# The candidate gate's tanh as an activation of its own, into PSUM, in a recurrence woven through a decoder kernel

## The reference, cut to what matters

```python
def step(carry, xg_t):
    h, c = carry
    g = xg_t + h @ W_hh.T
    i, f, gg, o = jnp.split(g, 4, axis=-1)
    c = jax.nn.sigmoid(f) * c + jax.nn.sigmoid(i) * jnp.tanh(gg)
    h = jax.nn.sigmoid(o) * jnp.tanh(c)
    return ((h, c), h)
```

## Time and profile before

| | us |
|---|---|
| median of 3 runs | 2719.52 |
| lowest, highest | 2716.49, 2726.72 |
| the profiled execution | 2719.7 |
| its span, first to last instruction | 2717.9 |
| PE busy in the span | 2429.8 (89%) |
| DVE busy | 1666.4 (61%) |
| ACT busy | 1296.7 (48%) |
| POOL busy | 1047.2 (39%) |

### The profile page before, as it was taken

The page is one execution under the profiler, slowest core; times in us unless marked ns, Lnnn a source line. Parts: engine busy times, 40 slices in busy tenths (PEclk is TensorE's granted clock), DMA queues, the critical chain, the costliest instruction groups (busy, mean ns, idle before and its releaser), DMA issues. The chain is left out here.

```text
span 2717.9 us, 42457 instructions
## 1 busy us (share of the span) xinstructions
PE 2429.8 (89%) x11677; PEld 1457.4 (54%) x11677; DVE 1666.4 (61%) x6007; ACT 1296.7 (48%) x4633; POOL 1047.2 (39%) x1124
## 2 busy tenths in 40 slices
PE   5799989989999898989999989898988888698887
PEld 2365645535546464636555555555545455466664
DVE  4446466676775766756676767676655646454541
ACT  0263636436364554536364646363543434366642
POOL 0223232122332433333333333333544544487665
PEclk9899999999899999989999999898998889798989
DMA  4301010100202011111202020303343222364324
GB/s 157 95 26 47 26 47 14 44 1 1 84 16 68 17 53 32 44 47 29 62 6 86 9 84 0 99 0 94 97 109 89 78 88 82 93 180 108 90 67 109
DMA packets 203623, 168.32 MB, mean 62 GB/s; under 512 B 56548, under 2 KB 196418, under 8 KB 203153
## 3 DMA queue, kind: packets, MB, share of 16 engines
q1 hardware_dynamic: 189072, 140.73, 17.9%
q0 software_dynamic: 14336, 25.28, 3.2%
HBM read 125.11 MB, written 53.40 MB: 66 GB/s over the span
## 5 line engine op out<-in xcount | busy, mean ns | idle before, releaser
L1163 ACT ACTIVATE l_scratch<-p,l_mx 128x64 f32<-128x64 f32 x2048 | 465.1, 306 | 29.6 <-DVE l_mx L1398 27.5
L951 PE MATMUL pg<-warm 128*64 128x512 bf16 x1528 | 424.7, 411 | 0.0
L1718 POOL TENSOR_TENSOR l_kbd<-l_kg,headmask 128x512 f32<-128x512 f32 x256 | 265.1, 1046 | 384.8 <-PE p L907 289.0
L1703 POOL TENSOR_TENSOR ln_rstd<-ln_ve,neghalf 128x4 f32<-128x4 f32 x96 | 98.2, 1023 | 628.7 <-DVE ln_ve L1360 627.2
L1644 DVE SCALAR_TENSOR_TENSOR uin<-gates 16x20 f32<-16x20 f32 x512 | 202.5, 395 | 206.9 <-ACT gates L1112 192.0
L931 PEld LDWEIGHTS p<-l_vg,l_scratch 128*128 128x128 f32 x2048 | 265.5, 200 | 60.5 <-issue 28.8
L1112 ACT ACTIVATE gates<-pg 16x80 f32<-16x80 f32 x512 | 113.2, 221 | 355.1 <-PE pg L940 343.4
L931 PE MATMUL p<-l_vg,l_scratch 128*128 128x34 f32 x2048 | 271.8, 281 | 8.8 <-ACT l_scratch L1171 4.3
L907 PE MATMUL p<-l_kbd,l_qT 128*128 128x512 f32 x512 | 272.0, 614 | 0.7 <-POOL l_kbd L1718 0.6
L951 PEld LDWEIGHTS pg<-warm 128*64 128x64 bf16 x1528 | 154.5, 115 | 186.5 <-issue 82.2
L940 PE MATMUL pg<-wcat,slots 128*16 128x80 f32 x1024 | 165.1, 244 | 96.7 <-DVE slots L1656 85.0
(11 more groups left out here) (287 smaller groups left out, 4479.2 us busy)
## 6 DMA issues: line engine op xcount, KB each, us to landing
xln<-xln_dram SPq DMA_DIRECT2D x40, 512.0 KB, 4.9
l_vg<-v_dram SPq DMA_DIRECT2D x32, 544.0 KB
x_dram<-l_xres SPq DMA_DIRECT2D x32, 512.0 KB, 4.9
l_kg<-k_dram SPq DMA_DIRECT2D x32, 256.0 KB, 4.2
xln_dram<-l_xnat SPq DMA_DIRECT2D x16, 512.0 KB, 3.9
l_xres<-x_dram SPq DMA_DIRECT2D x16, 512.0 KB
x_dram<-l_xnat SPq DMA_DIRECT2D x16, 512.0 KB
xin<-in_x SPq DMA_DIRECT2D x12, 512.0 KB, 3.8
```

What stands on the lines that cost most here:

```text
L951: pe.matmul(pg[64:128, :], warm[:, 0:64], warm[:, :], start=True, stop=True)
L1163: i = act.activation(w.ex[b % 2][:, NE * j + h, :], banks[lane][j][:, h * SK:(h + 1) * SK], ACT.Exp, scale=-1.0, bias=w.mx[:, u % 4, h:h + 1])
L1718: pool.tensor_tensor(w.kbd[b % 2][:, j, :, :], w.kg[:, j, b:b + 1, :].broadcast_to([P, NE, SK]), headmask[:, :].rearrange("p (a o) -> p a ...
```

## The change

The tanh of the candidate gate is cut out of the activation of all four gates. It gets an activation of its own, ahead of the other, which writes a new region `gate_in` of the PSUM tile `pg`. The other activation has 60 columns instead of 80 and alone signals the semaphore. `uin` reads its second input from `gate_in`. The regions `cell`, `ukept` and `tcell` move within `pg` (from multiples of 128 to multiples of 96) to make room. The planner's cost of the family `tanh` goes from 0.23 to 0.38.

```diff
@@ lstm_steps
-        steps += [("pe", "gates", s, 0.34, [...]), ("act", "tanh", s, 0.23, [("gates", s)]),
+        steps += [("pe", "gates", s, 0.34, [...]), ("act", "tanh", s, 0.38, [("gates", s)]),
@@ decoder_program
-        gates = sb("gates", [B, 4 * PE_])
+        gates = sb("gates", [B, 3 * PE_])
...
-        cell, ukept, tcell = (pg[0:B, j * P:j * P + PE_] for j in range(1, 4))
+        cell, ukept, tcell, gate_in = (pg[0:B, j * 96:j * 96 + PE_] for j in range(1, 5))
@@ act_lstm
                 if family == "tanh":
                     act.wait_ge(l_pe, k + s + 1)
-                    act.activation(gates[:, 0:80], pg[0:B, 0:80], ACT.Tanh).then_inc(l_tanh, 1)
+                    act.activation(gate_in[:, :], pg[0:B, 60:80], ACT.Tanh)
+                    act.activation(gates[:, 0:60], pg[0:B, 0:60], ACT.Tanh).then_inc(l_tanh, 1)
@@ dve_lstm
-                    dve.scalar_tensor_tensor(uin[:, :], gates[:, 0:20], 1.0, gates[:, 60:80], ALU.add, ALU.mult)
+                    dve.scalar_tensor_tensor(uin[:, :], gates[:, 0:20], 1.0, gate_in[:, :], ALU.add, ALU.mult)
```

More of the change, by code:

```diff
@@ L322, in lstm_steps @@
     for s in range(count):
-        steps += [("pe", "gates", s, 0.34, [("state", s - 1), ("slots", s // 8)]), ("act", "tanh", s, 0.23, [("gates", s)]),
+        steps += [("pe", "gates", s, 0.34, [("state", s - 1), ("slots", s // 8)]), ("act", "tanh", s, 0.38, [("gates", s)]),
                   ("dve", "cell", s, 0.5, [("tanh", s)]), ("act", "tcell", s, 0.15, [("cell", s)]),
```

## The result

The changed kernel takes 2641.5 us (median of 4 runs, 2632.5 to 2649.1) against 2718.2 for the kernel before (2716.5 to 2726.7): a ratio of 0.971 (95% interval 0.967 to 0.975), 77 us or 2.9% faster. On two more chips the ratio was 0.965 (0.960 to 0.970) and 0.968 (0.966 to 0.971).

The account below looks back on a forecast made before the run. TensorE's idle time of 165.7 us in the recurrence's four stages was taken as the most to win. 2719.7 - 49.9 (holding) + 8 (activation) + 0 (order) + 3 (stall) = 2680.8, so 2680 us on the median's scale; range 2650 to 2712.

Parts of the forecast that it names:

- What bounds the kernel: In the four recurrence stages a faster recurrence wins back at most TensorE's idle time, 165.7 us; fillers are fixed in number.
- The held time: Line 1644, held while GpSimd runs, loses its 117.0 us of holding once uin has one input in PSUM.
- How much of it is on the path: Of the 117.0 us held, TensorE's idle time behind the waits gives -49.9 us; the other 67 us change nothing.
- The added activation: On ScalarE, ahead of the signalling activation in every step, it delays gates: +8 us, bounds 4 to 71 us.
- Rival 3: The added activation is on the path at every step: up to 71 instead of 8 us, 2744 us; chance 0.05.
- The planner's cost: Tanh cost 0.38 makes the orders of stages 1 to 4 anew: taken as 0, about 15 us either way.
- rival 2: The new order is worse, +3 us in each of 14 bodies: 2723 us, at half that 2702; chance 0.15.
- Stall passed on: Other VectorE instructions with two SBUF inputs, as line 1376, are sometimes held by GpSimd instead: +3 us.
- Rival 1: The holding moves to VectorE's other two-input instructions, such as line 1376: +16 instead of +3, 2694 us; chance 0.12.
- Rival 4: uin is held in spite of its PSUM input: 2719.5 + 8 = 2728 us; chance 0.02.
- The check that the forecast proposed: Line 1644's longest under 200 ns, VectorE busy about 117 us less, TensorE idle about 40 us less in four stages.

Follow-up runs that it names:

- the old order: The change's instructions with the planner's tanh cost put back to 0.23, so order and fillers of the kernel before: 2617.1 us, 0.958 of the kernel before.
- the dead work: The change's instructions in the old order, plus an unneeded VectorE reduction ahead of uin once in eight steps: 2705.2 us, 0.998 of the kernel before.
- in SBUF: The kernel before, same order, with the candidate's tanh as its own activation into an SBUF tile, uin still held: 2743.4 us, 1.003 of the kernel before.
- the spread: The changed kernel, cost 0.38, with the spreads and windows the planner chose at 0.23: 2614.3 us, 0.966 of the kernel before.

## Why the prediction missed the size

*What bounds the kernel.* The forecast said that a faster recurrence can win back at most what TensorE idles, 165.7 us, since the number of fillers is fixed, and so priced the end of the holding, -49.9 us, by TensorE's idle time alone. This is the step that failed. The number of matmuls is fixed, but not their time: TensorE's busy time contains the lower clock that follows its pauses. In place of 49.9 us the old order's stretch gained 111.9, and 58.6 of them came out of busy time.

*The held time.* Right: 117 us of holding, gone from line 1644, with no instruction of a step held in its place. That this instruction is not held with one input in PSUM, as read from the earlier trace rows, is confirmed.

*How much of it is on the path.* The term of 49.9 us was counted as TensorE's idle time behind the waits, and as such it was near: the idle time fell by 53.3 us. Its bounds of 24 to 60 us, though, were bounds of idle time only, and the high end of the range left out the 15 us of the order besides. The busy time fell by as much again. The sentence that the remaining 67 us change nothing was wrong: the dead work shows that nearly all of VectorE's lost time is felt, 94 to 108 of 111.9 us.

*The added activation.* 8 us forecast; 8 us and 9 us (in SBUF) measured, each to some 6 us. The two durations, 138 and 193 ns, are as expected, and the second starts 0.08 us after the first. Rival 3 (63 us more) is ruled out.

*The planner's cost.* Taken as 0 with 15 us either way; it is +19.5 us in the changed kernel. It lay just outside what I kept for it and had the sign of rival 2. Why the new order is slower stays open. The expected cause, the spread, was tried and made no difference by itself; the 78 fillers more, with 25.3 us of TensorE's time, are a cause that no run tested. The orders differ in many other places too. The loss also hid part of the error: without it the forecast of 39 us would have stood against about 108.

*Stall passed on.* 3 us forecast, 2.7 us in line 1377, but that is luck. In the old-order kernel, where the recurrence is as free, the line has a mean of 398 ns, as before (399), so the 2.7 us belong to the new order. Rival 1 did not happen. Rival 4, that `uin` stays held, did not either.

The stretch of the changed kernel adds up as measured: 61.1 us less idle time and 21.2 us less busy time, 82.3 us in all. From the kernel before to the old order without holding the gain is 111.9 us, with the cost of the added activation in it, and the new order takes 29.6 back.

Behind the recurrence's last matmul the changed kernel takes 402.7 us instead of 391.0. In its profiles on two more chips it takes 405.1 and 385.8 us there, so the kernel alone does not set it. The windows of the kernel before, then of the changed one in its first profile and in the shortest:

```profile
2326.90:2717.90 391.00, 317.89 (x1645) 221.76 (x1645) 168.25 (x485) 189.38 (x598) 257.41 (x336) 0.90 0.37 106
```

```profile
2244.20:2646.90 402.70, 316.89 (x1635) 222.61 (x1635) 167.55 (x486) 189.00 (x599) 254.34 (x332) 0.88 0.36 103
```

```profile
2221.00:2606.80 385.80, 311.23 (x1625) 217.89 (x1629) 167.88 (x483) 188.73 (x596) 253.89 (x332) 0.91 0.37 108
```

The granted clock differs between the two, 0.88 and 0.91; why it does for one kernel is left open.

The check that the forecast proposed would have caught it in part: idle time was to fall by about 40 us, and fell by 61. What it did not ask for was TensorE's busy time at the same matmuls, and the granted clock by stage, 0.97 to 0.89 in the earlier trace rows and 0.94 in the mean, which already said that some 118 us (0.06 x 1968) were being paid to the clock in these stages.

## What to carry to other kernels

In this kernel, time that VectorE lost on the recurrence's chain came back in TensorE's time twice, once as idle time and again as a lower clock behind it. The price of 1 us lost was 0.8 to 1.05 us with fillers and 1.3 to 1.4 without, where TensorE's idle time alone said 0.43. So do not price a stall by TensorE's idle time alone, and look at span x (1 - mean clock) before saying what can be won. An instruction whose median is that of its neighbour and whose mean is not is worth a look at the longest single one: see whether its end falls on another engine's end. When an edit also changes a planner's cost, measure edit and order apart: here the old order with the new instructions is the fastest kernel on that chip, 2613.6 us, 0.960 of the kernel before, where the change as made gives 0.968 on the same chip.

## What the runs showed of the hardware

A VectorE instruction of 16 x 20 elements with both inputs in SBUF was held for up to 4.56 us, through three GpSimd instructions that followed one another without a pause, while the same instruction with one input in PSUM took 247 ns at the most in 512. A pause of TensorE of 3.8 us was followed by 10.2 us at the granted clock of 0.50, in which a pair of matmuls took 1.91 us instead of 1.02. 64 pieces of dead work of 1.75 us on VectorE brought the mean clock of the whole span from 0.957 to 0.943 with 40 us of extra matmul time. One more activation of 20 columns in each of the 512 steps, 0.12 to 0.14 us long, cost about 8 us, 16 ns a step.
